# Perceiver block on one core: small loads moved from ScalarE's to SyncE's queue, the first weights' low parts made partly on VectorE, TensorE padded at the start

## The reference, cut to what matters

```python
x = x + cross_attention(ctx_1024, layernorm(x), ...)   # 16 heads of 64, 4096 context rows + 256 own rows
x = x + performer_attention(layernorm(x), ...)
x = x + mixture_of_experts(layernorm(x), ...)          # 8 experts and a shared one

# cross attention
xn = layernorm(ctx, ln_x_g, ln_x_b)
ln = layernorm(latents, ln_l_g, ln_l_b)                # latents = layernorm(x)
q  = rmsnorm(ln @ Wq, qn_g) * 64**-0.5
k, v = split(concat([xn @ Wkv, ln @ Wkv]))
k = rmsnorm(k, kn_g)
out = softmax(q k^T) v ; return out @ Wout + bout
```

## Time and profile before

| what | value |
|---|---|
| time, median of 3 runs | 704.05 us (703.61 to 705.65) |
| profiled execution: its time | 703.4 us |
| profiled execution: span of the trace | 701.7 us |
| PE busy | 660.5 us (94% of the span) |
| DVE busy | 499.3 us (71%) |
| ACT busy | 417.2 us (59%) |
| POOL busy | 236.7 us (34%) |
| HBM read | 29.38 MB |
| first PE instruction | 12.93 us after the span's start |

### The profile page before, as it was taken

How to read it: one execution, slowest core, us unless ns; L and a number is a source line. 1 busy time by engine, 2 the same in 40 slices (tenths; PEclk the granted TensorE clock), 3 DMA queues, 4 the chain that set the end, 5 groups by cost and what they waited for, 6 DMA issues and landing times. The chain is left out here.

```text
span 701.7 us, 14395 instructions
## 1 busy us (share of the span) xinstructions
PE 660.5 (94%) x5152; PEld 526.8 (75%) x5152; DVE 499.3 (71%) x977; ACT 417.2 (59%) x878; POOL 236.7 (34%) x219
## 2 busy tenths in 40 slices
PE   1899999899999999999999999999998997899997
PEld 0777776677677777777777777777776886899997
DVE  2798898866867677687768767767676636867573
ACT  3687888656556666665666666566663313565650
POOL 3544434532233242222334332232220023355640
PEclk9999999999999999999999999999999989999999
DMA  5111460100000000000000000000002104256500
GB/s 161 36 56 32 123 182 1 46 1 2 1 16 16 2 31 1 2 1 16 1 2 1 1 2 1 16 2 1 1 2 68 53 1 164 78 196 218 166 19 16
DMA packets 26131, 30.50 MB, mean 43 GB/s; under 512 B 4169, under 2 KB 23762, under 8 KB 26066
## 3 DMA queue, kind: packets, MB, share of 16 engines
q1 hardware_dynamic: 23410, 28.79, 12.9%
q10 hardware_dynamic: 2656, 0.86, 0.5%
HBM read 29.38 MB, written 0.26 MB: 42 GB/s over the span
## 5 line engine op out<-in xcount | busy, mean ns | idle before, releaser
L796 POOL TENSOR_TENSOR k_rms<-k_ss,neg_half 128x4 f32<-128x4 f32 x136 | 137.1, 1008 | 312.6 <-DVE k_ss L689 312.6
L538 ACT ACTIVATE probs<-s_ps,minus_bound 128x512 f32<-128x512 f32 x272 | 164.6, 688 | 90.2 <-PE s_ps L386 90.2
L168 PE MATMUL kv_ps<-w_quad,xn 128*128 128x512 f32 x816 | 211.0, 405 | 1.6 <-issue 1.5
L683 DVE SCALAR_TENSOR_TENSOR probs_sum<-probs,tile_mask,probs_sum 128x512 f32<-128x512 f32 x264 | 192.4, 765 | 5.2 <-ACT probs L538 4.8
L168 PEld LDWEIGHTS kv_ps<-w_quad,xn 128*128 128x128 f32 x816 | 147.3, 188 | 45.0 <-issue 6.4
L399 PE MATMUL o_ps<-probs,v 128*64 128x256 f32 x1088 | 132.6, 385 | 0.8 <-ACT probs L538 0.7
L386 PEld LDWEIGHTS s_ps<-q_parts,kt 64*128 64x128 f32 x1632 | 101.1, 185 | 36.0 <-issue 19.6
L386 PE MATMUL s_ps<-q_parts,kt 64*128 64x256 f32 x1632 | 114.9, 287 | 9.2 <-DVE kt L693 9.2
L667 DVE SCALAR_TENSOR_TENSOR kn<-k_rms,kv_ps 128x256 f32<-128x256 f32 x136 | 56.7, 417 | 67.5 <-POOL k_rms L796 67.0
L399 PEld LDWEIGHTS o_ps<-probs,v 128*64 128x64 f32 x1088 | 72.0, 136 | 41.9 <-issue 10.7
L530 ACT ACTIVATE kt<-s_ps 128x256 fp32r<-128x256 f32 x136 | 44.9, 383 | 63.9 <-PE s_ps L372 63.6
(11 more groups left out here) (185 smaller groups left out, 666.7 us busy)
## 6 DMA issues: line engine op xcount, KB each, us to landing
w_raw<-in_ffn_W SPq DMA_DIRECT2D x18, 1024.0 KB, 5.2
rows<-in_ctx SPq DMA_DIRECT2D x8, 512.0 KB, 3.9
w_raw<-in_L_xattn_Wkv SPq DMA_DIRECT2D x6, 256.0 KB, 3.1
wout<-in_L_xattn_Wout SPq DMA_DIRECT2D x4, 256.0 KB, 2.7
wq_raw<-in_L_xattn_Wq SPq DMA_DIRECT2D x3, 256.0 KB, 3.3
w_raw<-in_L_xattn_Wkv ACTq DMA_DIRECT2D x2, 256.0 KB, 6.7
x_res<-in_x SPq DMA_DIRECT2D x1, 256.0 KB, 3.6
wq_raw<-in_L_xattn_Wq ACTq DMA_DIRECT2D x1, 256.0 KB, 4.1
```

Of the source, the lines that this page charges most:

```text
L168: last = nc.tensor.matmul(out, stationary(k, s), moving(k, m), start=n == 0, stop=n == len(terms) - 1)
L538: nc.scalar.activation(probs[n % P_RING][:, :, c, :], s_ps[n % 2][c][:], ACT.Exp, bias=minus_bound[:]).then_inc(exp_done, 1)
L683: nc.vector.scalar_tensor_tensor(total, probs[n % P_RING][:, :, c, :], seen, total, ALU.mult, ALU.add).then_inc(sum_done, 1)
L796: nc.gpsimd.tensor_tensor(k_rms[n % 2][:].rearrange("p i c -> p (i c)"), k_ss[n % 2][:].rearrange("p i c -> p (i c)"), neg_half[:, 0:4], A ...
```

## The change

It moves 11 small loads from ACT's DMA queue to SP's: the gains for `x` (two) go between the load of `x` and the first load of rows; the gains for the context, the query and key gains and the mask go between the first and the second load of rows. ACT no longer waits for all four gains first, but for each two where it uses them. ACT does an `Exp` on one column into an unread tile right after its three DMA issues, so that the function table is loaded there. ACT's hand-written order becomes center(0), queries_hi(0), gain(0), center(1), weights_hi(0), gain(1), square_q(0), center(2). The low part of `wq` for the first pass moves from POOL to DVE; that of `w_quad` is shared out, one half of the contraction (k = 0) on POOL, the other (k = 1) on DVE with a semaphore of its own, `w_lo_first`, for which PE waits before project(0). DVE's order becomes statistics(1), low part of `wq`, offset(1), rest(0), center(1), statistics(2), low part of `w_quad` (k = 1), rest(1), offset(2), center(2). PE does 20 matmuls of the identity with itself (128x128, into a bank that is not in use yet) before transpose_z(0), and 14 more before transpose_z(1).

```diff
 (SP)
             sp.dma_start(x_res[:], ...).then_inc(x_in, 16)
-            for g in range(1, 4):
+            with nc.allow_non_contiguous_dma(reason="a vector onto partitions"):
+                load_gains(0, gains_in)
+                load_rows(1)
+                load_gains(1, gains_x_in)
+                for n, name in enumerate(("qn_g", "kn_g")):
+                    for c in range(2):
+                        sp.dma_start(gq_col[c * DH:(c + 1) * DH, n:n + 1], ...).then_inc(gq_in, 16)
+                    sp.dma_start(gq[:, n, :], ...partition_broadcast(P)).then_inc(gq_in, 16)
+            sp.dma_start(mask_raw[:], a["mask_BxS2_bf1"]).then_inc(mask_in, 16)
+            for g in range(2, 4):
                 load_rows(g)
...
 (PE)
             pe.wait_ge(ident_done, 1)
+            keep_busy(nc, s_ps[1][1][:, 0, 0:P], ident[:], ident[:], 20)
             transpose_z(0)
+            keep_busy(nc, s_ps[1][1][:, 0, 0:P], ident[:], ident[:], 14)
             transpose_z(1)
             project_q(0)
             project(0)          # first waits for w_lo_first as well
...
 (ACT)
-            (11 dma_start of gains, gq, gq_col, mask_raw)
+            act.wait_ge(const_done, 1)
+            nc.scalar.activation(unread[:], neg_half[:, 0:1], ACT.Exp)
...
-            act.wait_ge(gains_in, 64)
             center(0)
+            queries_hi(0)
+            gain(0)             # waits for gains_in 32; gain(1) for gains_x_in 32
+            center(1)
             weights_hi(0)
-            center(1)
-            gain(0)
-            queries_hi(0)
             gain(1)
+            square_q(0)
             center(2)
-            square_q(0)
...
 (DVE)
             statistics(1)
+            dve.wait_ge(wq_hi, 1)
+            nc.vector.tensor_tensor(wq[:, :, 1, :], wq_raw[:], wq[:, :, 0, :].bitcast(F32), ALU.subtract).then_inc(wq_lo, 1)
             offset(1)
+            rest(0)
             center(1)
             statistics(2)
-            rest(0)
+            dve.wait_ge(w_hi, 1)
+            nc.vector.tensor_tensor(w_quad[0][:, 1, 1, :], w_raw[:, 1, :], w_quad[0][:, 1, 0, :].bitcast(F32), ALU.subtract).then_inc(w_lo_first, 1)
+            rest(1)
             offset(2)
             center(2)
...
-            rest(1)
             mean_square_q(0)
...
 (POOL)
+                k = 1 if g == 0 else KD
+                nc.gpsimd.tensor_tensor(w_quad[g % 2][:, 0:k, 1, :], ...)
...
             weights_lo(0)
-            queries_lo(0)
             root_of(2)
```

More of the change, by code:

```diff
@@ L194, in attention @@
         gains = ring(1, "gains", [P, 2, 2, KD])[0]
+        unread = ring(1, "unread", [P, 1])[0]
         gq, gqk = ring(1, "gq", [P, 2, DH])[0], ring(1, "gqk", [P, DH])[0]
@@ L223, in attention @@
         o_ps = [ctx.enter_context(nc.psum_tensor(f"o_ps{b}", [P, 2, NQ], F32)) for b in range(2)]
-        x_in, gains_in, gq_in, mask_in = sem("x_in"), sem("gains_in"), sem("gq_in"), sem("mask_in")
+        x_in, gains_in, gains_x_in, gq_in, mask_in = sem("x_in"), sem("gains_in"), sem("gains_x_in"), sem("gq_in"), sem("mask_in")
         rows_in = [sem(f"rows_in{b}") for b in range(3)]
@@ L236, in attention @@
         qt_done, qt_hi, qt_lo = sem("qt_done"), sem("qt_hi"), sem("qt_lo")
-        w_in, w_hi, w_lo = sem("w_in"), sem("w_hi"), sem("w_lo")
+        w_in, w_hi, w_lo, w_lo_first = sem("w_in"), sem("w_hi"), sem("w_lo"), sem("w_lo_first")
         wout_in, bout_in, bout_added = sem("wout_in"), sem("bout_in"), sem("bout_added")
@@ L289, in load_queries, with load_gains @@
                 sp.dma_start(wq_raw[:], wq_view(a)[t]).then_inc(wq_in, 16)
+            def load_gains(which, landed):
+                for n, name in enumerate(("ln_l_g", "ln_l_b", "ln_x_g", "ln_x_b")):
+                    if n // 2 == which:
+                        sp.dma_start(gains[:, which, n % 2, :], a["L0_xattn_" + name].rearrange("(k p) -> p k", p=P)).then_inc(landed, 16)
             sp.dma_start(x_res[:], a["x"].rearrange("o (j p) d -> p (o j) d", p=P)).then_inc(x_in, 16)
-            for g in range(1, 4):
+            with nc.allow_non_contiguous_dma(reason="a vector onto partitions"):
[4 more added lines that the diff above has]
+                    for c in range(2):
+                        sp.dma_start(gq_col[c * DH:(c + 1) * DH, n:n + 1], a["L0_xattn_" + name].rearrange("(p o) -> p o", o=1)).then_inc(gq_in, 16)
+                    sp.dma_start(gq[:, n, :], a["L0_xattn_" + name].partition_broadcast(P)).then_inc(gq_in, 16)
+            sp.dma_start(mask_raw[:], a["mask_BxS2_bf1"]).then_inc(mask_in, 16)
+            for g in range(2, 4):
                 load_rows(g)
@@ L316, in _ @@
                 sp.wait_ge(w_lo, g)
+                if g == 1:
+                    sp.wait_ge(w_lo_first, 1)
                 load_weights(g)
@@ L329, in project @@
                     pe.wait_ge(w_lo, g + 1)
+                if n == 0:
+                    pe.wait_ge(w_lo_first, 1)
                 if g == 0:
@@ L487, in gain @@
                 act.wait_ge(zt_done, u + 1)
+                if u == 0:
+                    act.wait_ge(gains_in, 32)
+                if u == 1:
+                    act.wait_ge(gains_x_in, 32)
                 if u >= 2:
@@ L800, in weights_lo @@
                 pool.wait_ge(w_hi, g + 1)
-                nc.gpsimd.tensor_tensor(w_quad[g % 2][:, :, 1, :], w_raw[:], w_quad[g % 2][:, :, 0, :].bitcast(F32),
+                k = 1 if g == 0 else KD
+                nc.gpsimd.tensor_tensor(w_quad[g % 2][:, 0:k, 1, :], w_raw[:, 0:k, :], w_quad[g % 2][:, 0:k, 0, :].bitcast(F32),
                                         ALU.subtract).then_inc(w_lo, 1)
```

## The result

| kernel | median us | runs | lowest to highest | ratio to the kernel before (95% interval) |
|---|---|---|---|---|
| before | 703.83 | 4 | 703.27 to 705.65 | |
| changed | 697.53 | 4 | 695.47 to 700.55 | 0.9906 (0.9887 to 0.9925) |
| changed, once more (e1) | 700.65 | 6 | 696.83 to 702.16 | 0.9942 (0.9921 to 0.9962) |

The second comparison gives 4.1 us (2.7 to 5.6). The times of the changed kernel also scatter over 5 us, those of the kernel before over 2.4.

What follows compares the result with a forecast made beforehand. TensorE is busy all the time from 60 us, so the chain to the first scores bounds the start; root_q moving from 22.36 to 17.55 gains 4.8 us: 704.05 - 4.8 = 699.25, forecast 699.2, range 697.4 to 701.9.

Steps and rivals of the forecast that it cites:

- The chain of the beginning: Steps on DVE and POOL before the first scores: root_q starts at 17.55 instead of 22.36, gain 4.8 us.
- The collision of DVE and POOL: Side-by-side subtractions share one port: rstd(1) at 11.05 instead of 10.45, DVE's half ends at 14.8 instead of 14.0.
- from there on the same intervals as before: After first scores near 25.4, everything behind keeps its old intervals; no further gain or loss.
- The sum: The start's steps added up: 4.8 us taken off the median, 704.05 - 4.8 = 699.25.
- a fall before the loop: Rival: PE's clock falls between project(1) and the keys' transposes, costing 2.4 us, 701.65; chance 0.06.
- the price of a pad: PE's identity matmuls at the start: 0.21 us each at first, so 20 end at 6.1, before z(0) at 7.5.
- one of my signs of being wrong: Listed signs: rows land past 10, pads run into z(0), or the loop's first turns show long matmuls.
- No collision: Rival: DVE and POOL don't meet, or rows come at 7.7; gain 5.7, both 6.4: 698.35 to 697.65; chance 0.18.
- Small loads in front of the rows: Rival: each microsecond the rows land after 8.4 costs one; at 12.3 the time is 703.15; chance 0.13.
- Pads as the bound: Rival: pads cost 0.44 us each, the clock level doesn't rise, query projection ends at 22.0; 705.15; chance 0.03.

Runs made afterwards that it cites:

- e8: The changed kernel with both low parts (of `wq` and `w_quad`) back on POOL, none on DVE; one run, 700.90 us.
- e4: The changed kernel without the 34 pads (matmuls of the identity); median 695.68 us, ratio 0.9884.
- e15: The changed kernel without the 34 pads, measured once more; median 697.09 us, ratio 0.9886.
- e2: The kernel before with only the unused one-column tile allocated behind the gains, moving later tiles by 32 bytes; median 700.65 us, ratio 0.9954.
- e13: The kernel before with 32 bytes allocated ahead of `w_quad` and 32 behind it, so `w_quad` lies on byte 164864; one run, 700.03 us.
- e3: The changed kernel with the one-column tile allocated last, so all other tiles lie as before the change; median 700.19 us, ratio 0.9946.
- e5: The changed kernel without the 34 pads and with the one-column tile allocated last; median 699.47 us, ratio 0.9925.
- e10: The kernel before with 64 unused bytes allocated behind the gains, moving `w_quad` to byte 164896; median 703.91 us, ratio 0.9994.
- e14: The kernel before with 32 bytes allocated right behind `w_quad`, moving only the tiles behind it; one run, 703.67 us.
- e7: The changed kernel with the first load of rows ahead of the two gain loads for `x` on SP's queue; one run, 696.60 us.
- e6: The kernel before with the 34 pads added at the same two places; median 705.29 us over 12 runs, ratio 1.0004.
- e9: The changed kernel without the 34 pads and with the first rows ahead of the gains for `x`; median 699.32 us, ratio 0.9916.
- e12: The changed kernel without pads, with rows ahead of the gains and POOL's later low parts in four pieces; median 696.53 us, ratio 0.9892.
- e11: The changed kernel with POOL's low part of the next pass's weights in four instructions instead of one; median 696.90 us, ratio 0.9892.

## Why the prediction was right or wrong

**Where it was right.** The chain of the beginning on DVE and POOL came step by step as forecast: the rows at 8.79 (I took 8.4), rstd(1) ready for the offset at 11.33 (11.1), DVE's half of the weights until 15.0 (14.8), offset(2) 16.20 (15.8 to 16.25), root_q 17.78 (17.4 to 17.9), first scores 25.63 (near 25.4). The gain there is 4.63 us against 4.8. The collision of DVE and POOL, the one place where I let a row and the Trainium skill's SBUF — State Buffer, section "SBUF: two separate sides", weigh against the change, is there at both places: 0.58 and 1.72 us. e8 shows it the other way round, 1.21 us. The pads give next to nothing at the first scores, as forecast (e4, e15).

**The step that failed** is "from there on the same intervals as before". The sum has no term for where the tiles lie. The unread tile counted for nothing in it, though it shifts every tile behind it. It moves `w_quad` from an odd multiple of 32 bytes to a multiple of 64, and that makes passes 2 to 4 shorter by 1.3 us (355.8 against 357.1; e2 and e13 against e3, e5, e10 and e14). With the same falls of the clock the change is worth 4.6 + 1.3 = 5.9 us, not 4.8.

**The second step that failed** was to let the sum stand against the median as if the clock after 30 us were the same in each execution. I named a fall before the loop (2.4 us, chance 0.06); e1 shows one that cost 1.8 us, e8 another of 1.6. But the falls behind the 2.0 us gap of the first pass and in the performer cost 1.5 and up to 3.3 us and come and go between executions of one kernel. The first four runs had mean clocks of 0.985 to 0.995, e1's six had 0.983 to 0.993: 6.6 and 4.1 us by the ratios, on both sides of 5.9. So how far a median lies from the forecast is partly luck. The profiled execution gained only 2.85 us because its clock was low for longer: 3.4 us more in the first pass cost 1.4 us, and 3.4 more in the performer cost 1.7. The 3.4 more in the experts show no cost, 119.7 us in both kernels.

**A third step, wrong without harm: the price of a pad.** I took 0.21 us for each of the 20 and let them end at 6.1. The rows of 128 columns are 0.21 us apart at the lower level indeed, but a call of `keep_busy` makes two of them, so a pad costs 0.43 us there and 0.22 at the higher level. The earlier trace rows could have told it: its 18 matmuls are the call `keep_busy(..., 9)` of the printed kernel. That the pads run into z(0) was one of my signs of being wrong, and they did, by 1.2 us. It cost nothing at the first scores, because rest(0) on DVE started at 11.41, when the high part it needs had been there since 10.87.

**The rivals.** No collision: wrong. Small loads in front of the rows: the rows landed at 8.79, which is 0.39 us after the 8.4 I took, and 0.23 of that is left at root_q (17.78 against 17.55). Against e7, with the rows first, the small loads cost 1.54 us at the landing and 1.76 at the first scores. Pads as the bound: wrong for the changed kernel, but its price of 0.44 us a pad was right; only its condition failed, that the clock doesn't rise. The clock rose at 6.3 us. In e6, where it fell again, the pads were the bound.

**What stays open.** Why a multiple of 64 bytes brings the projection's matmuls closer together isn't shown. That it does rests on one such address, 164864, against two odd multiples of 32. Nor is it shown what decides in an execution whether the clock falls: each of the nine falls seen in the first pass stood behind the 2.0 us gap, and six traces with that gap have no fall. Before the first scores the clock fell in two of the six traces of the new beginning with pads (e1, e8) and in none of the five without (e4, e5, e9, e12, e15), which is too few to blame the pads. That the ratios of e4 and e15 agree (0.9884, 0.9886) and lie below that of e1 hints at a cost of the pads through the clock; e6 against the kernel before and e9 don't bear it out.

## What to carry to other kernels

Follow the chain to the start of the loop step by step, but compare the tiles' addresses of both kernels too: a tile of 4 bytes can be worth more than the instruction that fills it. Where DVE and POOL share work, put the short operation that someone waits for outside the other's long one, or cut the long one in pieces, and count what the pieces cost on their own engine. Before pricing a helper by its rows, count how many rows one call leaves. When runs of one kernel differ by more than the change, read the granted clock of each stretch and compare stages at equal clock before explaining a median.

## What the runs showed of the hardware that I had not expected

- The weights that the matmuls of 512 columns stream lay at byte 164864 of a partition instead of 164832 (or 164896): 355.5 to 355.9 us instead of 356.9 to 357.2 for three passes, and 230 instead of 233 ns from one start to the next.
- With matmuls of the identity from 1.9 us on the clock rose between 4.8 and 7.6 us in seven traces; in e6 it fell again at 11.8 while PE waited. Falls from the first pass to the experts last 3.4, 6.8 or 10.2 us.
- POOL's subtraction of 512 elements held a one-element DVE operation for 1.2 us (0.16 alone), as DVE's held POOL's two-element one (0.58 against 0.2). POOL's subtraction in four pieces let DVE's operation through in 1.22 us instead of 2.86 (e11).
- Two loads of 256 packets of 4 bytes ahead of 512 KB on the same queue delayed its landing by 1.5 us (8.79 against 7.25 in e7).
